# A recurrence step rearranged: one gate TANH, one spread, two f16 parts, and an f32 score product

## The chip, the cores and the metric

The kernel runs on one core of a Trainium2 chip. The metric is the device time of one launch in microseconds (us); lower is better. The kernel before took 1523.16 us, the median of three runs (1520.36 to 1537.06).

## The reference, cut to what matters

The reference is two layers over x of shape (4, 256, 512): attention over a context of 64 positions, a feed-forward with int4 weights, then a recurrent attention decoder, then a mixture of 16 experts. The decoder is a scan over the 256 positions, and each step needs the state of the one before:

```
f = conv1d(alpha, conv_w)                       # alpha: last step's attention over 64 positions
e = va . tanh(enc_proj + s @ Wa_s.T + f @ Wa_f.T + ba);  masked
alpha_new = softmax(e);   g = alpha_new @ hbatch
rec = tgt @ L_ys.T + s @ L_ss.T + g @ L_gs_w.T + L_gs_b
ig, fg, cg, og = split(rec, 4)
c_next = sig(fg) * c + sig(ig) * tanh(cg);  s_next = sig(og) * tanh(c_next)
```

Here sig(z) = 0.5 tanh(z/2) + 0.5, the batch is 4 and s, c have 64 elements each. The output y of the step is computed later from the kept histories of s and alpha.

## The kernel before, in words

Attention and the first part of the feed-forward run ahead of the recurrence. After about 302 us the 256 steps begin. The rest of the feed-forward, the inputs of the gates, the outputs and most of the experts are cut into small pieces, and `fill(...)` puts such pieces between the parts of a step on each engine. Every engine has its own instruction stream, written out by hand, in order; semaphores join them.

On TensorE a step is: the state's share of the tanh argument (L1864, high part `sh`, then low part `sl`), the state's share of the gates (L1870: five small products for each of two gate halves, over three bf16 parts of L_ss), a fill, the score maxima `eb` (L1878: eight 32-column products of `th_hi`), the exact scores `et` (L1884 twice, a fill, then L1887, three 8-column products with `th_hi` and `th_lo` as weights), a fill, the gates and sums from the exponentials (L1896, L1901, L1905, L1912, L1913), the context for the next step (L1618, three bf16 parts), the masks (L1612, L1613), a fill, the f32 convolution product (L1921, two products that each show as two instructions) and a last fill.

ScalarE makes two TANH of the 128x128 argument (L1425 to f16, L1426 to f32), two EXP (L1430, L1431), two TANH of the gates on 64 partitions each (L1439, L1440) and one of the cell (L1442). VectorE makes the state sum `rs`, `th_lo` (L1095), the maximum (L1098), `el` (L1103), the reciprocal (L1106), two normalisations, the gate sum (L1117), the spread in two halves (L1121, each with a semaphore), `ab` (L1130), the cell (L1132), `sh`, `s2` and `sl` (L1135, L1136, L1138). GpSimd copies the state (L689), does a piece of fill after `th_lo_ready`, and writes the attention history after the reciprocal.

A fill is counted in half units: a product of 256 columns is 1, one of 512 columns is 2. A credit is carried from fill to fill, so a 512-column product may overdraw it by 1 and the next fill pays. In a step the fills before `eb`, between L1884 and L1887, before L1896, before L1921 and at the end have 2, 2, 4, 4 and 3 half units. Where no work is due, `keep_busy` (L1842) issues one product of as many columns, with 384 instead of 512 for 2 half units in the first fill.

Of the kernel before, what the change touches and what calls it, by code (L numbers as in the profile page):

```python
# [17 lines left out]
P = 128  # L18
# [13 lines left out]
J = 64  # L32
# [8 lines left out]
def shape_constants():  # L41
# [6 lines left out]
    for m in range(NF // 2 + 1):  # L48
# [28 lines left out]
        "c_gatescale": np.stack([np.where(np.arange(P) < J, 1.0, 2.0), np.ones(P)], 1).astype(f32),  # L77
# [5 lines left out]
def build(nc, a, out):  # L83
    with ExitStack() as ctx:
# [31 lines left out]
        identb = sb("identb", [P, P], BF16)  # L116
# [5 lines left out]
        lss3 = sb("lss3", [J, 3, 256], BF16)  # L122
# [8 lines left out]
        vae2 = sb("vae2", [P, 2, 2 * B], F16)  # L131
# [6 lines left out]
        enc3 = sb("enc3", [P, 3, P], BF16)  # L138
# [28 lines left out]
        tfi = sb("tfi", [J, 8])  # L167
        xs = sb("xs", [J, 2, 12])
        ab = sb("ab", [J, 8])
        tc_sb = sb("tc_sb", [J, B])  # L170
# [13 lines left out]
        th_hi = ker_mem[:, 256:320].bitcast(F16)  # L184
        th_lo = ker_mem[:, 320:384].bitcast(F16)
# [69 lines left out]
        def w1_piece(q):  # L255
# [17 lines left out]
            pre_done th_s th_full th_lo_ready eb_done et_done mx_ready eh_ready ex_ready el_ready sum_done ah_done hg_done rinv_ready ahn_ready  # L273
            prod_ready g_ready q0_ready q1_ready kept tg_ready ab_ready c_ready tc_ready s_ready sh_ready sl_ready sp_done
            identb_ready hist_done part_ready
# [244 lines left out]
        def _(pool):  # L520
# [82 lines left out]
            nc.gpsimd.memset(xs[:], 0.0)  # L603
# [14 lines left out]
            nc.gpsimd.tensor_copy(identb[:], ident[:]).then_inc(s["identb_ready"], 1)  # L618
# [66 lines left out]
            for l in range(S):  # L685
# [4 lines left out]
                pool.wait_ge(s["th_lo_ready"], l + 1)  # L690
# [15 lines left out]
        def _(dve):  # L706
# [157 lines left out]
            in_parts(lss3[:], lssT[:])  # L864
# [4 lines left out]
            in_halves(vae2[:], vae[:].rearrange("p h b -> p (h b)"))  # L869
# [4 lines left out]
            in_parts(enc3[:], enc[:])  # L874
# [211 lines left out]
            for l in range(S):  # L1086
# [42 lines left out]
                dve.wait_ge(s["tg_ready"], l + 1)  # L1129
                nc.vector.scalar_tensor_tensor(ab[:], tfi[:], 1.0, xs[:, par, 0:8], ALU.add, ALU.mult).then_inc(s["ab_ready"], 1)  # L1130
# [338 lines left out]
        def _(pe):  # L1469
# [542 lines left out]
```

## Time and profile before

| | |
|---|---|
| runs (us) | 1520.36, 1523.16, 1537.06 |
| the profiled execution's own time | 1518.94 us |
| its span | 1516.8 us |
| busy share PE, PEld, DVE, ACT, POOL | 92%, 61%, 62%, 36%, 18% |
| mean granted TensorE clock | 0.93 |

PE is TensorE's matmuls, PEld its weight loads, DVE is VectorE, ACT is ScalarE, POOL is GpSimd. Matmuls are pipelined and their ends are modelled, so that a PE that shows as busy may still be waiting for its next weight load; where that happens it is seen as idle time of PEld.

### The profile page before, as it was taken

The page shows a single profiled execution, that of the slowest core. Times are in us where ns is not written, and L with a number is a line of the kernel's source. Part 1 is how long each engine was busy: PE and PEld are TensorE (multiplying, and loading weights), DVE is VectorE, ACT ScalarE, POOL GpSimd, SP SyncE. Part 2 cuts the span into 40 slices and gives each one's busy share as a digit, 9 for nine tenths or more (in the row PEclk, how much of TensorE's full clock was granted, in tenths as well). Part 3 has the DMA queues.
Part 4 walks back from the last instruction along what each step waited for, and adds up shares of the span by engine and source line. Part 5 has one row for each costly group of instructions (what it writes and reads, how often), then busy time and mean ns, then how long its engine had stood idle before and what let it go on. Part 6 is the DMA issues. An engine that isn't in the chain of part 4 may idle for free.

```text
span 1516.8 us, 43579 instructions
## 1 busy us (share of the span) xinstructions
PE 1395.5 (92%) x17408; PEld 919.4 (61%) x17408; DVE 943.9 (62%) x4478; ACT 544.3 (36%) x2143; POOL 275.1 (18%) x743
## 2 busy tenths in 40 slices
PE   4743887899999999999999999999999999999988
PEld 2533666466665676666666765556666666666546
DVE  4898455366665666675666657766655566566643
ACT  1343132134333344333334434443433333333321
POOL 3334222211111111111011111231110011111111
PEclk8565797999999999999999999999998999999989
DMA  8623000000000000000000001210000000000000
GB/s 278 240 90 90 0 1 4 1 2 2 3 2 2 2 2 2 3 2 2 2 2 2 2 19 45 58 37 2 2 16 2 2 2 9 9 2 3 9 9 14
DMA packets 19551, 37.06 MB, mean 24 GB/s; under 512 B 8436, under 2 KB 11683, under 8 KB 19348
## 3 DMA queue, kind: packets, MB, share of 16 engines
q1 hardware_dynamic: 19348, 34.28, 6.9%
q8 instruction: 136, 2.23, 0.6%
q14 instruction: 67, 0.55, 0.1%
HBM read 32.18 MB, written 2.10 MB: 23 GB/s over the span
## 4 chain that ended last, share of the span: by engine, by line
PE 83%; DVE 9%; issue 3%; ACT 2%; SPq 1%; POOL 1%; DMA 0%; DVEq 0%; ACTq 0%; POOLq 0%
PE bank L1921 9%; PE bank L1842 9%; PE bank L1635 9%; PE bank L1864 8%; PE bank L1652 6%; PE bank L1896 6%; PE bank L1673 4%; PE bank L1870 4%; PE bank L1618 3%; PE bank L1878 3%; PE bank L1905 3%; PE bank L1884 2%; PE bank L1612 2%; PE bank L1566 2%; PE bank L1518 2%
## 5 line engine op out<-in xcount | busy, mean ns | idle before, releaser
L1842 PE MATMUL bank<-ctx_lgs,identb 128*128 128x512 f16 (+2 forms) x685 | 190.9, 356 | 0.0
L1921 PE MATMUL bank<-ker_mem,uh 128*128 128x128 f32 x1020 | 184.3, 304 | 0.7 <-DVE ker_mem L1121 0.4
L1921 PEld LDWEIGHTS bank<-ker_mem,uh 128*128 128x128 f32 x1020 | 137.0, 194 | 66.1 <-DVE ker_mem L1121 48.9
L1635 PE MATMUL bank<-xT,wbig 128*128 128x256 f16 x1008 | 162.9, 275 | 0.0
L693 POOL TENSOR_TENSOR sscale<-ex,rinv 128x8 f32<-128x8 f32 x256 | 51.0, 199 | 506.8 <-DVE rinv L1106 506.8
L1439 ACT ACTIVATE xs<-gat 64x8 f32<-64x8 f32 x255 | 52.9, 207 | 244.2 <-DVE gat L1117 244.2
L1425 ACT ACTIVATE ker_mem<-bank 128x128 f16<-128x128 f32 x256 | 71.0, 278 | 184.8 <-PE bank L1864 184.8
L1430 ACT ACTIVATE eh<-bank,nmx 128x8 f16<-128x8 f32 x256 | 68.5, 268 | 172.4 <-PE bank L1887 172.4
L689 POOL COPY sscale<-s 64x4 f32<-64x4 f32 x256 | 59.0, 230 | 388.6 <-DVE s L1136 388.6
L1652 PE MATMUL bank<-wbig,interT 128*128 128x512 f16 x378 | 125.6, 399 | 0.0
L1121 DVE TENSOR_TENSOR ker_mem<-inv,ahn 128x128 f32<-128x128 f32 x510 | 124.0, 285 | 0.1
L1896 PEld LDWEIGHTS bank<-eh,ctx_lgs 128*128 128x128 f16 x2048 | 69.3, 96 | 69.9 <-ACT eh L1430 69.3
L1103 DVE TENSOR_TENSOR el<-ex,eh 128x8 f16<-128x8 f32 x256 | 42.9, 168 | 103.9 <-ACT ex L1431 103.7
L1092 DVE TENSOR_TENSOR rs<-bank,rin 128x8 f32<-128x8 f32 x256 | 42.6, 166 | 95.6 <-PE bank L1870 95.3
L1518 PE MATMUL bank<-vbd,interT 128*128 128x34 f32 x256 | 51.0, 361 | 49.2 <-ACT interT L1203 49.2
L1106 DVE RECIPROCAL rinv<-bank 128x4 f32<-128x4 f32 x256 | 46.6, 182 | 78.2 <-PE bank L1905 78.2
L1896 PE MATMUL bank<-eh,ctx_lgs 128*128 128x4 f16 x2048 | 90.3, 166 | 2.0
L1864 PEld LDWEIGHTS bank<-sh,was 64*128 64x128 f16 x512 | 28.4, 94 | 102.8 <-DVE sh L1135 98.8
L1442 ACT ACTIVATE tc_sb<-xs 64x4 f32<-64x4 f32 x255 | 52.4, 205 | 105.5 <-DVE xs L1132 105.5
L1095 DVE TENSOR_TENSOR ker_mem<-enc,ker_mem 128x128 f16<-128x128 f32 x256 | 74.8, 292 | 21.0
L1870 PE MATMUL bank<-sh,lss 64*128 64x4 f16 x1536 | 87.4, 162 | 0.0
L573 POOL TENSOR_TENSOR interT<-work,interT 128x256 f16<-128x256 f32 x84 | 56.2, 670 | 164.5 <-ACT interT L1214 93.3
(238 smaller groups left out, 3290.9 us busy)
## 6 DMA issues: line engine op xcount, KB each, us to landing
wbig<-d_gate_qT SPq DMA_DIRECT2D x4, 896.0 KB, 9.9
wbig<-d_up_qT SPq DMA_DIRECT2D x4, 896.0 KB, 20.7
wbig<-d_down_qT SPq DMA_DIRECT2D x1, 3584.0 KB, 31.5
x_sb<-d_x SPq DMA_DIRECT2D x16, 128.0 KB, 6.0
d_out<-x_sb SPq DMA_DIRECT2D x16, 128.0 KB, 2.3
sscale<-d_gate_sT SPq DMA_DIRECT2D x2, 896.0 KB, 8.3
sscale<-d_up_sT SPq DMA_DIRECT2D x2, 896.0 KB, 4.3
work<-d_g1T SPq DMA_DIRECT2D x8, 224.0 KB, 2.5
```

What stands on the lines that cost most here:

```text
L1095: nc.vector.tensor_tensor(th_lo, th, th_hi, ALU.subtract).then_inc(s["th_lo_ready"], 1)
L1121: return nc.vector.tensor_tensor(qv[:, h, :, :], inv[:].unsqueeze(1).broadcast_to([P, B, TH]), ahn[:, 4 * h:4 * h + 4].unsqueeze(2).broadc ...
L1425: nc.scalar.activation(th_hi, bank[0][:, 0:P], ACT.Tanh).then_inc(s["th_s"], 1)
L1430: nc.scalar.activation(eh[:], bank[0][:, P:P + 8], ACT.Exp, bias=nmx[:, 0:1]).then_inc(s["eh_ready"], 1)
L1518: last = mm(bank[6 + pair // 8][:, (pair % 8) * 34:(pair % 8) * 34 + 34], pT[:, n % 2, j * P:(j + 1) * P], vbd[:, b, pair // 2, :], start= ...
L1635: last = mm(tile_bank(n)[:, lo:lo + QC], w[wi][:, kt, it * P:(it + 1) * P], x_part[q % 2][xi][:, kt, :], start=(kt == 0 and wi + xi == 0), ...
L1652: last = mm(bk[:], i_part[ii][:, it, p * P:(p + 1) * P], w[wi][:, it, :], start=(it == 0 and ii + wi == 0), stop=(it == tiles - 1 and ii = ...
L1842: mm(bank[7][:, 0:n], identb[:], hg2[:, 0].rearrange("p h g -> p (h g)")[:, 0:n], start=True, stop=True)
L1864: last = mm(bank[0][:, 0:P], was2[:, j, :], st[:].unsqueeze(2).broadcast_to([J, B, TH]), start=False, stop=(st is sl), skip_group_check=True)
L1870: last = mm(bank[2][:, 4 * gp:4 * gp + 4], lss3[:, j, gp * P:(gp + 1) * P], st[:], start=(gp == 0 and j == 0 and st is sh), stop=(j == 1 a ...
L1896: mm(bank[2][:, 8 + 4 * gp:12 + 4 * gp], hg2[:, j, h, gp * P:(gp + 1) * P], e[:, 4 * h:4 * h + 4], start=False, stop=final, skip_group_che ...
L1921: mm(bank[0][:, 0:P], uh[:, h, :], qv[:, h, :, :], start=False, stop=False, skip_group_check=True)
```

## The change

The order of the gates is now i, f, c, o, as in the reference, so that one TANH over 128 partitions (into `tg`) gives all four; `ab` is made by two instructions, one on each half of the partitions. The spread is one VectorE instruction of 256 columns with one semaphore. L_ss and the context are held in two f16 parts instead of three bf16 parts. There is one TANH of the argument, in f32 (`th`); its upper two bytes, read as bf16 with a step of two, feed the maxima, and `th` itself is the weights of a single f32 score product, ahead of the fill. The fills of a TensorE step are 3, 5, 4 and 3 half units. The wait on `kept` moves from the second spread to `s2`; GpSimd's fill waits for `mx_ready`.

```diff
-            def in_parts(dst, src):
-
-                for j in range(2):
-                    link(nc.vector.tensor_copy(dst[:, j], src))
-                    link(nc.vector.tensor_tensor(src, src, dst[:, j], ALU.subtract))
-                nc.vector.tensor_copy(dst[:, 2], src).then_inc(s["part_ready"], 1)
...
-            in_parts(lss3[:], lssT[:])
+            in_halves(lss2[:], lssT[:])
...
-            in_halves(vae2[:], vae[:].rearrange("p h b -> p (h b)"))
...
-            in_parts(enc3[:], enc[:])
+            in_halves(enc2[:], enc[:])
...
+        th_top = th.bitcast(BF16).rearrange("p (n two) -> p two n", two=2)[:, 1, :]
...
-                pool.wait_ge(s["th_lo_ready"], l + 1)
+                pool.wait_ge(s["mx_ready"], l + 1)
...
-                dve.wait_ge(s["th_full"], l + 1)
-                nc.vector.tensor_tensor(th_lo, th, th_hi, ALU.subtract).then_inc(s["th_lo_ready"], 1)
-
...
-                spread(0).then_inc(s["q0_ready"], 1)
+                nc.vector.tensor_tensor(qv.rearrange("p i b t -> p (i b) t"), inv[:].unsqueeze(1).broadcast_to([P, 2 * B, TH]),
+                                        ahn[:].unsqueeze(2).broadcast_to([P, 2 * B, TH]), ALU.mult).then_inc(s["q_ready"], 1)
+
+                dve.wait_ge(s["tg_ready"], l + 1)
+                nc.vector.scalar_tensor_tensor(ab[J:P, 0:4], tg[0:J, par, 0:4], 1.0, tg[0:J, par, 4:8], ALU.add, ALU.mult)
+                nc.vector.scalar_tensor_tensor(ab[J:P, 4:8], tg[J:P, par, 0:4], 1.0, cell[J:P, par, :], ALU.add, ALU.mult).then_inc(s["ab_ready"], 1)
+                dve.wait_ge(s["ab_ready"], l + 1)
+                nc.vector.scalar_tensor_tensor(cell[J:P, 1 - par, :], ab[J:P, 4:8], 0.5, ab[J:P, 0:4], ALU.mult, ALU.add).then_inc(s["c_ready"], 1)
...
                 dve.wait_ge(s["kept"], l + 1)
-                spread(1).then_inc(s["q1_ready"], 1)
...
-                nc.scalar.activation(th_hi, bank[0][:, 0:P], ACT.Tanh).then_inc(s["th_s"], 1)
                 nc.scalar.activation(th, bank[0][:, 0:P], ACT.Tanh).then_inc(s["th_full"], 1)
...
-                nc.scalar.activation(xs[:, par, 4:12], gat[J:P, :], ACT.Tanh, scale=0.5)
-                nc.scalar.activation(tfi[:], gat[0:J, :], ACT.Tanh, scale=0.5).then_inc(s["tg_ready"], 1)
+                nc.scalar.activation(tg[:, par, :], gat[:], ACT.Tanh, scale=0.5).then_inc(s["tg_ready"], 1)
...
-                for j in range(3):
-                    mm(bank[0][:, 0:P], identb[:], enc3[:, j, :], start=(j == 0), stop=False, skip_group_check=True)
+                for j in range(2):
+                    mm(bank[0][:, 0:P], identh[:], enc2[:, j, :], start=(j == 0), stop=False, skip_group_check=True)
...
-                    for j, st in ((0, sh), (1, sh), (2, sh), (0, sl), (1, sl)):
+                    for j, st in ((0, sh), (1, sh), (0, sl)):
...
-                fill(UNIT, main_first, 384)
-                pe.wait_ge(s["th_s"], l + 1)
+                fill(UNIT + HALF_UNIT, main_first, 384)
+                pe.wait_ge(s["th_full"], l + 1)
...
-                        last = mm(bank[1][b * TH:(b + 1) * TH, h * TH:(h + 1) * TH], vah[:, h, :], th_hi[:, b * TH:(b + 1) * TH],
+                        last = mm(bank[1][b * TH:(b + 1) * TH, h * TH:(h + 1) * TH], vah[:, h, :], th_top[:, b * TH:(b + 1) * TH],
...
-                pe.wait_ge(s["th_full"], l + 1)
-                for j in range(2):
-                    mm(bank[0][:, P:P + 8], th_hi, vae2[:, j, :], start=False, stop=False, skip_group_check=True)
-                fill(UNIT, main_first)
-                pe.wait_ge(s["th_lo_ready"], l + 1)
-                mm(bank[0][:, P:P + 8], th_lo, vae2[:, 0, :], start=False, stop=True, skip_group_check=True).then_inc(s["et_done"], 1)
-
-                fill(2 * UNIT, side_first)
+                mm(bank[0][:, P:P + 8], th, vae[:].rearrange("p h b -> p (h b)"), start=False, stop=True, skip_group_check=True).then_inc(s["et_done"], 1)
+
+                fill(2 * UNIT + HALF_UNIT, side_first)
...
+                pe.wait_ge(s["q_ready"], l + 1)
                 for h in range(2):
-                    pe.wait_ge(s[f"q{h}_ready"], l + 1)
                     mm(bank[0][:, 0:P], uh[:, h, :], qv[:, h, :, :], start=False, stop=False, skip_group_check=True)
                 fill(UNIT + HALF_UNIT, side_first)
```

## Rows read from the trace of the kernel before

**Rows 1.** Page: granted clock, group of L1121 (busy us, mean ns); then the reciprocal's line.

```profile
PEclk8565797999999999999999999999998999999989
...
L1121 DVE TENSOR_TENSOR ker_mem<-inv,ahn 128x128 f32<-128x128 f32 x510 | 124.0, 285 | 0.1
...
L1106 DVE RECIPROCAL rinv<-bank x256: 181/182/184, 304.4 to 1466.1; 128x4 f32<-128x4 f32 x128
```

**Rows 2.** Timeline (start us, us, engine line op [idle before]): spread, gates, state.

```profile
800.60 0.49 DVE L1121 TENSOR_TENSOR ker_mem<-inv,ahn 128x128 f32<-128x128 f32 x2
800.71 0.21 ACT L1439 ACTIVATE xs<-gat 64x8 f32<-64x8 f32 x1 [0.87 <-DVE gat L1117]
...
800.93 0.52 PEld L1921 LDWEIGHTS bank<-ker_mem,uh 128*128 128x128 f32 x4
...
801.17 0.16 DVE L1130 SCALAR_TENSOR_TENSOR ab<-tfi,xs 64x8 f32<-64x8 f32 x1
801.37 0.15 DVE L1132 SCALAR_TENSOR_TENSOR xs<-ab 64x4 f32<-64x4 f32 x1
...
801.49 0.49 PE L1635 MATMUL bank<-xT,wbig 128*128 128x256 f16 x3
...
801.79 0.15 DVE L1135 SCALAR_TENSOR_TENSOR sh<-xs,tc_sb 64x4 f16<-64x4 f32 x1 [0.27 <-ACT tc_sb L1442]
...
802.00 0.11 PEld L1864 LDWEIGHTS bank<-sh,was 64*128 64x128 f16 x2 [0.31 <-DVE sh L1135]
...
802.13 0.42 DVE L897 SCALAR_TENSOR_TENSOR work<-work,bank 128x256 f32<-128x256 f32 x1
802.26 0.09 PEld L1864 LDWEIGHTS bank<-sl,was 64*128 64x128 f16 x1
```

**Rows 3.** Timeline of the same step: argument, maxima, scores, exponentials; the next spread.

```profile
802.53 0.28 ACT L1425 ACTIVATE ker_mem<-bank 128x128 f16<-128x128 f32 x1 [0.77 <-PE bank L1864]
...
802.65 0.39 PE L1635 MATMUL bank<-xT,wbig 128*128 128x256 f16 x2
...
802.98 0.13 PEld L1878 LDWEIGHTS bank<-ker_mem,vah 128*32 128x32 bf16 x8 [0.21 <-ACT ker_mem L1425]
...
803.14 0.11 PEld L1884 LDWEIGHTS bank<-vae,ker_mem 128*128 128x128 f16 x2
...
803.28 0.23 DVE L1098 TENSOR_REDUCE nmx<-bank 128x1 f32<-128x64 f32 x1
...
803.43 0.17 PE L1887 MATMUL bank<-vae,ker_mem 128*128 128x8 f16 x1
...
803.63 0.27 ACT L1430 ACTIVATE eh<-bank,nmx 128x8 f16<-128x8 f32 x1 [0.66 <-PE bank L1887]
...
803.95 0.27 PEld L1896 LDWEIGHTS bank<-eh,ctx_lgs 128*128 128x128 f16 x8 [0.18 <-ACT eh L1430]
...
804.31 0.11 PEld L1905 LDWEIGHTS bank<-el,onesb 128*128 128x128 bf16 x2
...
805.09 0.49 DVE L1121 TENSOR_TENSOR ker_mem<-inv,ahn 128x128 f32<-128x128 f32 x2
```

**Rows 4.** Timeline of the first step, whose first fill is one product of 384 columns.

```profile
302.44 0.28 ACT L1425 ACTIVATE ker_mem<-bank 128x128 f16<-128x128 f32 x1 [1.14 <-PE bank L1864]
...
302.56 0.34 PE L1842 MATMUL bank<-ctx_lgs,identb 128*128 128x384 f16 x1
...
302.83 0.13 PEld L1878 LDWEIGHTS bank<-ker_mem,vah 128*32 128x32 bf16 x8 [0.17 <-ACT ker_mem L1425]
```

**Rows 5.** Timeline: four f32 products of 16 columns in the router, eight weight loads.

```profile
710.27 0.97 PEld L1757 LDWEIGHTS bank<-gwT,kbd 128*128 128x128 f32 x8
```

**Rows 6.** Timeline of VectorE: reciprocals, six microseconds apart.

```profile
716.43 0.18 DVE L1106 RECIPROCAL rinv<-bank 128x4 f32<-128x4 f32 x1 [0.56 <-PE bank L1905]
...
722.39 0.18 DVE L1106 RECIPROCAL rinv<-bank 128x4 f32<-128x4 f32 x1 [0.55 <-PE bank L1905]
```

**Rows 7.** Timeline ahead of the recurrence: the down projection on TensorE.

```profile
284.83 8.74 PE L1581 MATMUL bank<-wbig,interT 128*128 128x512 f16 x38
```

More of the change, by code:

```diff
@@ L76, in shape_constants @@
         "c_time2": np.stack([np.tile(np.arange(TH), B), np.tile(np.arange(TH, T), B)]).astype(f32),
-        "c_gatescale": np.stack([np.where(np.arange(P) < J, 1.0, 2.0), np.ones(P)], 1).astype(f32),
+        "c_gatescale": np.stack([np.ones(P), np.where(np.arange(P) < J, 2.0, 1.0)], 1).astype(f32),
         "c_batchsel": (bm[None] == four).astype(f32),
@@ L166, in build @@
         sl = sb("sl", [J, B], F16)
[L167 to L170, printed above, removed]
+        tg = sb("tg", [P, 2, 8])
+        cell = sb("cell", [P, 2, B])
+        ab = sb("ab", [P, 8])
+        tc_sb = sb("tc_sb", [P, B])
         s2 = sb("s2", [J, 2, B])
@@ L272, in build @@
             vbd_zero wsel_zero setup_v setup_mm setup_cp mask_ready scale_ready
-            pre_done th_s th_full th_lo_ready eb_done et_done mx_ready eh_ready ex_ready el_ready sum_done ah_done hg_done rinv_ready ahn_ready
-            prod_ready g_ready q0_ready q1_ready kept tg_ready ab_ready c_ready tc_ready s_ready sh_ready sl_ready sp_done
-            identb_ready hist_done part_ready
+            pre_done th_full eb_done et_done mx_ready eh_ready ex_ready el_ready sum_done ah_done hg_done rinv_ready ahn_ready
+            prod_ready g_ready q_ready kept tg_ready ab_ready c_ready tc_ready s_ready sh_ready sl_ready sp_done
+            identh_ready hist_done part_ready
             split_high split_done gated upped stat_ready top_ready y_done u_ready yy_done lg_done lgx_ready pe_exp wsel_ready wt_done wT_ready wT_low_ready expert_ready""".split()
@@ L593, in _ @@
             pool.wait_ge(s["setup_in"], 16 * SETUP)
-            nc.gpsimd.tensor_scalar(lssT[:, 0:J], lssT[:, 0:J], 0.5, None, ALU.mult)
-            nc.gpsimd.tensor_scalar(lssT[:, 2 * J:4 * J], lssT[:, 2 * J:4 * J], 0.5, None, ALU.mult)
+            nc.gpsimd.tensor_scalar(lssT[:, 0:2 * J], lssT[:, 0:2 * J], 0.5, None, ALU.mult)
+            nc.gpsimd.tensor_scalar(lssT[:, 3 * J:4 * J], lssT[:, 3 * J:4 * J], 0.5, None, ALU.mult)
             nc.gpsimd.tensor_scalar(lsyT[:], lsyT[:], 0.5, None, ALU.mult)
             nc.gpsimd.tensor_scalar(wasT[:], wasT[:], 0.5, None, ALU.mult)
-            nc.gpsimd.tensor_scalar(lgsT[:, J:2 * J], lgsT[:, J:2 * J], 2.0, None, ALU.mult).then_inc(s["scale_ready"], 1)
+            nc.gpsimd.tensor_scalar(lgsT[:, 2 * J:3 * J], lgsT[:, 2 * J:3 * J], 2.0, None, ALU.mult).then_inc(s["scale_ready"], 1)
             rstd_of(10)
             rstd_of(11)
-            nc.gpsimd.memset(xs[:], 0.0)
+            nc.gpsimd.memset(cell[:], 0.0)
             nc.gpsimd.memset(s2[:], 0.0).then_inc(s["s_ready"], 1)
@@ L1606, in _ @@
             pe.wait_ge(s["rin_ready"], 2)
-            pe.wait_ge(s["part_ready"], 5)
-            pe.wait_ge(s["identb_ready"], 1)
+            pe.wait_ge(s["part_ready"], 4)
+            pe.wait_ge(s["identh_ready"], 1)
             def masks():
@@ L1840, in keep_busy @@
             def keep_busy(n):
-                mm(bank[7][:, 0:n], identb[:], hg2[:, 0].rearrange("p h g -> p (h g)")[:, 0:n], start=True, stop=True)
+                mm(bank[7][:, 0:n], identh[:], hg2[:, 0].rearrange("p h g -> p (h g)")[:, 0:n], start=True, stop=True)
             credit = [0]
@@ L1984 @@
     ctx = i["ctx_1024"]
-    perm = np.concatenate([np.arange(q * J, (q + 1) * J) for q in (1, 2, 0, 3)])
     kT = ctx.reshape(B, T, 8, HD).transpose(2, 3, 0, 1)
```

34 lines of the change are left out of this document (12 added, 22 removed).

## The prediction

> **What bounds the kernel now.** I read the page's row of granted clocks and the reciprocal's line first [rows 1]: one reciprocal a step, 256 from 304.4 to 1466.1 us, so 1161.7 us in 255 steps, 4.556 us each. The recurrence is 77% of the span, and what is saved in a step is multiplied by 255. The second view is the timeline of one step, between two spreads: 805.09 - 800.60 = 4.49 us [rows 2, 3]. The page says that PE is 92% busy, but much of that is fill, and the weight loads tell another story: L1864 sat idle 0.31 us until VectorE's `sh`, L1878 0.21 us until the TANH, L1896 0.18 us until the EXP [rows 2, 3]. So a step is a loop through four engines, in which TensorE's fills are nearly as long as the waits that they stand in. A shorter link helps only until the fill beside it is the longer one, and I price both at each place.
>
> **Gates.** Before, the first TANH starts at 800.71, the second after it, and `ab` starts at 801.17 [rows 2]. Now one TANH ends at 800.71 + 0.21 = 800.92 (8 columns on twice the partitions; bounds 0.20 and L1425's 0.28 for 128 columns), `tg` is there at 800.95. VectorE must also be done with the spread. Two halves of 0.285 took 0.49 us together [rows 1, 2], so neighbours on VectorE overlap by 0.08. A 128x256 f32 instruction takes 0.42 (L897) [rows 2]: the spread ends at 801.02, the first `ab` starts at 800.95, the second 0.08 later (upper bound: a whole 0.16). `c` starts 0.04 after the second has ended: 800.95 + 0.08 + 0.16 + 0.04 = 801.23, against 801.37. All behind it, TANH of the cell, `sh`, `s2`, `sl`, moves with it: **0.14 us**. The wait on `kept` ahead of `s2` costs nothing: the copy that it waits for was started when the last state was written, nearly a step ago.
>
> What TensorE does beside it: L1921 started at 800.93, 0.05 after the first half spread; it now waits for the whole, 801.02 + 0.05 = 801.07, **0.14 us later**. Its four instructions and the way into the fill took 801.49 - 800.93 = 0.56 us, so the last fill starts at 801.63. A 256-column product takes 0.11 us (0.49 for three, 0.39 for two [rows 2, 3]), three take 0.32: streamed out at 801.95. The new `sh` is on TensorE at 801.86, so L1864's first products start 0.09 late; but `sl`, whose load was at 802.26 and is possible now at 802.12, comes after two 128-column products, at 801.95 + 0.11 = 802.06. So the low part still sets the end, and the 0.14 stays whole, with 0.06 us to spare. With two 512-column products in the last fill (every other step of a 512-column stretch) the end is 0.11 later and 0.05 of the 0.14 is lost.
>
> If the spread takes as long as the halves did one after the other without overlap (2 x 0.285 = 0.57, upper bound [rows 1]), everything behind it moves 0.15 more, the margin is gone and the gain is 0.05; if it took 0.35 it would still be 0.14, for then the TANH sets it.
>
> **Argument and maxima.** L1870 goes from ten small products to six. They ran between L1864's low part and the fill, at about 0.035 us each: the fill starts 0.14 earlier. It is 3 half units instead of 2, +0.11: it ends 0.03 earlier. That matters: the first maxima start 0.17 us after the TANH's end behind two 256-column products (802.98 - 802.81 [rows 3]), but 0.11 behind one of 384 columns (302.83 - 302.72 [rows 4]). So **0.03 us** gained, 0.01 in steps of dummy fill; in 512-column stretches, where the first fill is now one or two products in turn, +0.07 and -0.07. The f32 TANH alone takes what the f16 one did. Reading `th` with a step of two costs the moving side between nothing and a doubling of eight times 32 columns, 0.11 us; I take nothing.
>
> **Scores.** Before, EXP starts 0.65 us after the maxima's first load, on L1887's end, 803.60; the maximum itself was done at 803.51 [rows 3]. `th_lo`'s wait and the fill in between made L1887 the last. Now the f32 product's loads start where L1884's did, 0.16 behind the maxima's. No row shows it; four f32 products of 16 columns take eight loads in 0.97 us [rows 5], 0.11 a load after a first of 0.19. Two loads are 0.30, and the second product's way out adds 0.10: done at 0.16 + 0.40 = 0.56, EXP at 0.60. Bounds: one f16 product's load and way out, 0.27, where the maximum would set EXP at 0.58; and twice the loads, 0.62, EXP at 0.82. At 0.60, **0.05 us** are gained. On TensorE the f32 product lets the fill of 5 half units start at 0.16 + 0.26 = 0.42 and end at 0.95; L1896 would be ready at 0.60 + 0.32 = 0.92 against 0.97 before. So some 0.03 to 0.05 arrive; I count 0.04. Three 512-column products there end at 1.06 and take back the 0.07 won before the maxima.
>
> The Trainium skill, page FP8 and Floating Point Precision, TensorE Precision Notes, gives a true FP32 product four passes through the array. By that rule, if each pass had its own load, the product would end 0.22 us later and the sum below would be near nothing; rows 5 show two loads a product, and the rival "dear product" carries the difference.
>
> **Costed at nothing.** The third context product is 0.05 us of TensorE between L1913 and the masks, which wait for the reciprocal anyway. `th_lo` leaves VectorE before the maximum, which waited for L1878. GpSimd's fill starts 0.2 us later, when the maximum is done; its next instruction needs the reciprocal, more than 1 us later. Nobody waits in the step for either. The eight VectorE instructions gone from the set-up, none of more columns than L897's, ran beside or ahead of the down projection, 8.74 us of unbroken TensorE [rows 7].
>
> **The sum.** Fill of 256 columns or dummy: 0.14 + 0.03 + 0.04 = 0.21. Fill of 512 columns: 0.14 and 0.09 in turn, 0.11. Of the 15 x 255 = 3825 half units, the two down projections in the loop are 378 products of 512, 756 half units, 20%. Mean 0.8 x 0.21 + 0.2 x 0.11 = 0.19; x 255 = 48 us. The mean step is 4.556 and the plain one 4.49, 17 us in all, mostly in a few steps that TensorE or a long fill sets; a tenth off for those: **44 us**. The profiled execution's own time 1518.94 becomes 1475. The median of the runs shown is 4.2 above it and the lowest 1.4; I put the median at **1477**.
>
> **Rivals.** (a) *TensorE takes it back*: one spread makes the convolution product late and the fills stay at 15 half units in a shorter step. For it: only 0.06 us of margin at `sl`, 0.03 at L1896. Against it: both margins are positive at the measured 0.42. With the upper spread 0.05 + 0.03 + 0.02 = 0.10 a step are left, 25 us: about 1494. (b) *Dear product*: the f32 loads double, EXP goes to 0.82 instead of 0.65 after the maxima and the gates' 0.14 is eaten: 1517, no change. Rows 5 speak against it. (c) *Slower, by the clock*: a step with the granted clock at half takes 722.39 - 716.43 = 5.96 us [rows 6], 1.5 more than a plain one. That stretch came after a step whose fill was the narrow f32 products of rows 5, where TensorE did less. The change takes ten small products and one of 128 columns out and puts weight loads of f32 in. If more steps fall to 1.2 GHz, 30 of them cost the whole gain and 42 make it 1% slower, about 1538. Against it: the same fill stands in a step 4% shorter, so per microsecond TensorE does no less than before, and most slices show nine tenths or more [rows 1]. (d) *It doesn't bite*: if `sl` or EXP hung on something else I have not seen, 1519.
>
> **Chances.** Forecast 0.68 (1463 to 1488), (a) 0.18, (b) 0.05, (c) 0.05, (d) 0.04. Within 1% of before, 1508 to 1538, is what a measurement can't tell from no change. Faster by over 1%: 0.68 + 0.18 less a little = 0.85; same: 0.10; slower 0.05. The range takes in (a): 1461 to 1502.
>
> **What would show it.** In the changed trace: plain steps of 4.28 us; `c` 0.63 after the spread's start against 0.77; spread 0.42; L1921's first load 0.47 after the spread's start; idle before L1864 nearly gone; EXP 0.60 after the maxima's first load; f32 score product two loads; as few slices below full clock as before. A spread near 0.57, a product of four loads, or L1896 later than 0.97 after the maxima would prove me wrong, in that order of likelihood.

## The result: slower by 1.3%, not faster by 3%

| | before | after |
|---|---|---|
| median of the runs (4 each) | 1528.12 us | 1546.95 us (1542.30 to 1551.83) |
| ratio, with its 95% interval | | 1.0128 (1.0079 to 1.0178) |
| profiled execution's own time | 1518.94 us | 1542.94 us |
| its span | 1516.8 us | 1541.2 us |
| mean granted clock | 0.93 | 0.93 |

I predicted 1477 us, a range of 1461 to 1502, and 5% for slower.

The profile after loses next to nothing outside the recurrence: first reciprocal at 304.63 us (304.4 before), last at 1490.16 (1466.1 before, [rows 1]), so 23.9 of the 24.4 us of span are in the 255 steps. I call a step under 4.8 us plain. Paired step by step, the 220 steps that are plain in both traces lose 15.8 us together, and the other 35 lose 8.1 us.

Where the plain steps lose is seen when each is cut at four points. Counted from one `sh` to the next (219 plain pairs, 15.5 us), the maxima's start costs 8.7 us, the way from there to EXP gives 8.7 back, the way from EXP to the spread costs 5.3, and the way from the spread to the cell costs 9.6. So there are three losses: the gates, the first fill, and one between EXP and spread. All three are taken in turn below, and the long steps with the experiments.

A table of medians over the plain steps, sorted by what the first fill is, shows the first two. Offsets are from the start of `sh`, in us:

| first fill, kernel | maxima's first load | EXP | spread | cell | step |
|---|---|---|---|---|---|
| 256-column products, before | 1.18 | 1.84 | 3.29 | 4.06 | 4.49 |
| same, after | 1.20 | 1.83 | 3.29 | 4.10 | 4.53 |
| 512-column products, before | 1.19 | 1.85 | 3.30 | 4.08 | 4.50 |
| same, after | 1.32 | 1.95 | 3.40 | 4.22 | 4.65 |
| dummy products, before | 1.12 | 1.78 | 3.24 | 4.00 | 4.43 |
| same, after | 1.12 | 1.74 | 3.20 | 4.01 | 4.44 |

The page after, first the clock row and the groups of the parts that I had priced. A group line gives the count, then the busy us in all and the mean ns of one, then the idle time ahead of them:

```profile
PEclk8565797999999999998999999999998999999998
...
L1421 ACT ACTIVATE tg<-gat 128x8 f32<-128x8 f32 x255 | 53.2, 209 | 252.0 <-DVE gat L1104 252.0
...
L1107 DVE TENSOR_TENSOR ker_mem<-inv,ahn 128x256 f32<-128x256 f32 x255 | 106.8, 419 | 0.2
...
L1863 PE MATMUL bank<-vae,enc 128*128 128x8 f32 x512 | 100.1, 268 | 0.0
```

All three prices were right: the TANH over 128 partitions 0.21, the spread 0.42, the f32 product two instructions. Now the timeline of one step after, with a fill of 256-column products (start us, us, engine, line, operation):

```profile
801.52 0.42 DVE L1107 TENSOR_TENSOR ker_mem<-inv,ahn 128x256 f32<-128x256 f32 x1
801.64 0.21 ACT L1421 ACTIVATE tg<-gat 128x8 f32<-128x8 f32 x1 [0.88 <-DVE gat L1104]
801.97 0.16 DVE L1111 SCALAR_TENSOR_TENSOR ab<-tg 64x4 f32<-64x4 f32 x1
801.99 0.52 PEld L1897 LDWEIGHTS bank<-ker_mem,uh 128*128 128x128 f32 x4 [0.30 <-DVE ker_mem L1107]
...
802.14 0.16 DVE L1112 SCALAR_TENSOR_TENSOR ab<-tg,cell 64x4 f32<-64x4 f32 x1
802.33 0.16 DVE L1114 SCALAR_TENSOR_TENSOR cell<-ab 64x4 f32<-64x4 f32 x1
...
802.76 0.16 DVE L1117 SCALAR_TENSOR_TENSOR sh<-tg,tc_sb 64x4 f16<-64x4 f32 x1 [0.27 <-ACT tc_sb L1423]
802.84 0.15 DVE L1119 SCALAR_TENSOR_TENSOR s<-tg,tc_sb 64x4 f32<-64x4 f32 x1
...
803.24 0.09 PEld L1845 LDWEIGHTS bank<-sl,was 64*128 64x128 f16 x1 [0.16 <-DVE sl L1121]
...
803.51 0.28 ACT L1408 ACTIVATE enc<-bank 128x128 f32<-128x128 f32 x1 [0.78 <-PE bank L1845]
...
803.53 0.50 PE L1616 MATMUL bank<-xT,wbig 128*128 128x256 f16 x3
...
803.96 0.13 PEld L1859 LDWEIGHTS bank<-enc,vah 128*32 128x32 bf16 x8 [0.21 <-ACT enc L1408]
...
804.13 0.30 PEld L1863 LDWEIGHTS bank<-vae,enc 128*128 128x128 f32 x2
804.13 0.39 PE L1863 MATMUL bank<-vae,enc 128*128 128x8 f32 x2
...
804.27 0.23 DVE L1085 TENSOR_REDUCE nmx<-bank 128x1 f32<-128x64 f32 x1 [0.46 <-PE bank L1859]
...
804.59 0.27 ACT L1412 ACTIVATE eh<-bank,nmx 128x8 f16<-128x8 f32 x1 [0.80 <-PE bank L1863]
```

Read it against rows 2. The TANH is done at 801.85, but the first `ab` starts at 801.97: not before the spread's end (801.94), though L1117 and L1121 of before had overlapped with their forerunners. The second `ab` starts 0.17 later, when the first is over; `sh` and `s2` (L1119, shown as `s`) are 0.08 apart in the same trace. So the cell comes 0.81 us after the spread's start, against 0.77 in [rows 2]; I had written 0.63. TensorE is where I said: L1897's first load 0.47 behind the spread's start.

The second loss is at the first fill, and largest in the stretches of 512-column fill:

```profile
1447.27 0.28 ACT L1408 ACTIVATE enc<-bank 128x128 f32<-128x128 f32 x1 [0.78 <-PE bank L1845]
...
1447.30 0.63 PE L1633 MATMUL bank<-wbig,interT 128*128 128x512 f16 x2
...
1447.85 0.13 PEld L1859 LDWEIGHTS bank<-enc,vah 128*32 128x32 bf16 x8 [0.45 <-ACT enc L1408]
```

The TANH is done at 1447.55; two products of 512 columns stand in front of the maxima, which start 0.30 behind it (0.17 in [rows 3]).

The third loss comes from GpSimd's fill, which now waits for the maximum (`mx_ready`) and no longer for `th_lo`. The groups of `el` on the two pages, before and after:

```profile
L1103 DVE TENSOR_TENSOR el<-ex,eh 128x8 f16<-128x8 f32 x256 | 42.9, 168 | 103.9 <-ACT ex L1431 103.7
```

```profile
L1090 DVE TENSOR_TENSOR el<-ex,eh 128x8 f16<-128x8 f32 x256 | 47.9, 187 | 95.4 <-ACT ex L1413 95.4
```

One step of each with such a piece of fill on GpSimd, before and after:

```profile
606.66 0.67 POOL L573 TENSOR_TENSOR interT<-work,interT 128x256 f16<-128x256 f32 x1 [1.12 <-DVE ker_mem L1095]
...
607.37 0.17 DVE L1103 TENSOR_TENSOR el<-ex,eh 128x8 f16<-128x8 f32 x1 [0.26 <-ACT ex L1431]
```

```profile
611.74 0.67 POOL L571 TENSOR_TENSOR interT<-work,interT 128x256 f16<-128x256 f32 x1 [1.33 <-DVE nmx L1085]
...
612.21 0.22 DVE L1090 TENSOR_TENSOR el<-ex,eh 128x8 f16<-128x8 f32 x1 [0.22 <-ACT ex L1413]
```

Before, GpSimd's instruction is over (607.33) when `el` starts. After, it ends at 612.41, and `el` ends 0.02 behind it and takes 0.22 us instead of 0.17. In the changed kernel's trace `el` takes over 0.20 us in 74 of 256 steps and ends 0.02 to 0.03 behind GpSimd in each of them; before, in 1. The spread starts 1.51 us after EXP where `el` overlaps GpSimd's fill, and 1.46 elsewhere. Of the sixteen traces, the twelve with the new wait have 71 to 76 such steps each, and the four with the old one (before, gates_only, parts_only, parts_22453) have 1 each. No run moves this wait alone.

### The profile page after: what moved, and what is told of

The parts are those of the page before. It is cut to its first block, busy times and chain, and to the rows that moved or that the text cites. A ratio compares the mean times of both kernels' runs of the same rounds, so it can differ in the third digit from the quotient of the medians.

```text
span 1541.2 us, 39817 instructions
## 1 busy us (share of the span) xinstructions
PE 1418.7 (92%) x15914; PEld 914.2 (59%) x15914; DVE 901.2 (58%) x4214; ACT 452.7 (29%) x1632; POOL 276.1 (18%) x743
## 4 chain that ended last, share of the span: by engine, by line
PE 83%; DVE 10%; issue 3%; ACT 1%; SPq 1%; POOL 1%; DMA 1%; DVEq 0%; ACTq 0%; POOLq 0%
PE bank L1897 12%; PE bank L1823 9%; PE bank L1616 8%; PE bank L1845 7%; PE bank L1633 6%; PE bank L1872 5%; PE bank L1863 5%; PE bank L1654 4%; PE bank L1859 3%; PE bank L1593 3%; PE bank L1881 3%; PE bank L1851 2%; PE bank L1599 2%; PE bank L1499 2%; PE bank L1547 2%
## 5 line engine op out<-in xcount | busy, mean ns | idle before, releaser
L1897 PEld LDWEIGHTS bank<-ker_mem,uh 128*128 128x128 f32 x1020 | 137.6, 195 | 105.4 <-DVE ker_mem L1107 105.2
L1897 PE MATMUL bank<-ker_mem,uh 128*128 128x128 f32 x1020 | 185.6, 306 | 6.4 <-DVE ker_mem L1107 2.8
L1823 PE MATMUL bank<-ctx_lgs,identh 128*128 128x512 f16 (+3 forms) x727 | 190.1, 346 | 0.0
L1085 DVE TENSOR_REDUCE nmx<-bank 128x1 f32<-128x64 f32 x256 | 57.5, 225 | 126.5 <-PE bank L1859 126.5
L1421 ACT ACTIVATE tg<-gat 128x8 f32<-128x8 f32 x255 | 53.2, 209 | 252.0 <-DVE gat L1104 252.0
L1408 ACT ACTIVATE enc<-bank 128x128 f32<-128x128 f32 x256 | 71.0, 277 | 181.9 <-PE bank L1845 181.9
L1107 DVE TENSOR_TENSOR ker_mem<-inv,ahn 128x256 f32<-128x256 f32 x255 | 106.8, 419 | 0.2
L1090 DVE TENSOR_TENSOR el<-ex,eh 128x8 f16<-128x8 f32 x256 | 47.9, 187 | 95.4 <-ACT ex L1413 95.4
L1423 ACT ACTIVATE tc_sb<-cell 64x4 f32<-64x4 f32 x255 | 51.6, 202 | 174.2 <-DVE cell L1114 174.2
L1863 PE MATMUL bank<-vae,enc 128*128 128x8 f32 x512 | 100.1, 268 | 0.0
L1616 PEld LDWEIGHTS bank<-xT,wbig 128*128 128x128 f16 x1008 | 85.8, 102 | 11.1 <-issue 1.2
## 6 DMA issues: line engine op xcount, KB each, us to landing
wbig<-d_gate_qT SPq DMA_DIRECT2D x4, 896.0 KB, 10.1
```

Source lines behind the costliest of these rows:

```text
L1107: nc.vector.tensor_tensor(qv.rearrange("p i b t -> p (i b) t"), inv[:].unsqueeze(1).broadcast_to([P, 2 * B, TH]), ahn[:].unsqueeze(2).broa ...
L1408: nc.scalar.activation(th, bank[0][:, 0:P], ACT.Tanh).then_inc(s["th_full"], 1)
L1616: last = mm(tile_bank(n)[:, lo:lo + QC], w[wi][:, kt, it * P:(it + 1) * P], x_part[q % 2][xi][:, kt, :], start=(kt == 0 and wi + xi == 0), ...
L1823: mm(bank[7][:, 0:n], identh[:], hg2[:, 0].rearrange("p h g -> p (h g)")[:, 0:n], start=True, stop=True)
L1863: mm(bank[0][:, P:P + 8], th, vae[:].rearrange("p h b -> p (h b)"), start=False, stop=True, skip_group_check=True).then_inc(s["et_done"], 1)
L1897: mm(bank[0][:, 0:P], uh[:, h, :], qv[:, h, :, :], start=False, stop=False, skip_group_check=True)
```

## The experiments

### The gates alone

```diff
 before, plus:
-                nc.scalar.activation(xs[:, par, 4:12], gat[J:P, :], ACT.Tanh, scale=0.5)
-                nc.scalar.activation(tfi[:], gat[0:J, :], ACT.Tanh, scale=0.5).then_inc(s["tg_ready"], 1)
+                nc.scalar.activation(tg[:, par, :], gat[:], ACT.Tanh, scale=0.5).then_inc(s["tg_ready"], 1)
-                nc.vector.scalar_tensor_tensor(ab[:], tfi[:], 1.0, xs[:, par, 0:8], ALU.add, ALU.mult)...
+                nc.vector.scalar_tensor_tensor(ab[J:P, 0:4], tg[0:J, par, 0:4], 1.0, tg[0:J, par, 4:8], ALU.add, ALU.mult)
+                nc.vector.scalar_tensor_tensor(ab[J:P, 4:8], tg[J:P, par, 0:4], 1.0, cell[J:P, par, :], ALU.add, ALU.mult)...
```

> The kernel before with the new gates alone (one TANH over 128 partitions, two instructions for ab), the spread still in two halves. Theory H (VectorE does not overlap an instruction with its neighbour when the start partition of an operand changes, so the second ab costs a whole instruction and the first waits for the spread's end): ab starts 0.52 us after the spread, the cell 0.88 against 0.77, a plain step 4.60 instead of 4.49, the kernel about 25 us slower than before. Theory S (the gates are fine and the single spread or the f32 product is at fault): the second ab starts 0.08 after the first, plain step 4.45 to 4.50, no slower than before.

Measured: 1573.72 us median, ratio 1.0234 (1.0144 to 1.0323). Plain steps 4.61. VectorE in one step:

```profile
802.99 0.49 DVE L1121 TENSOR_TENSOR ker_mem<-inv,ahn 128x128 f32<-128x128 f32 x2
803.10 0.21 ACT L1440 ACTIVATE tg<-gat 128x8 f32<-128x8 f32 x1 [0.84 <-DVE gat L1117]
803.50 0.15 DVE L1130 SCALAR_TENSOR_TENSOR ab<-tg 64x4 f32<-64x4 f32 x1
803.67 0.16 DVE L1131 SCALAR_TENSOR_TENSOR ab<-tg,cell 64x4 f32<-64x4 f32 x1
803.87 0.16 DVE L1133 SCALAR_TENSOR_TENSOR cell<-ab 64x4 f32<-64x4 f32 x1
```

0.51, 0.68 and 0.88 behind the spread, as theory H had it. With the spread in halves the new gates are dearer still. The plain steps lose what H said, 24.6 us in 205 of them. The other 50 lose 30.0 us more, which no theory had: the mean granted clock is below 0.9 in 29 steps, before in 9.

### The same instructions, reading from the same partition

```diff
 after, plus:
-                nc.vector.scalar_tensor_tensor(ab[J:P, 0:4], tg[0:J, par, 0:4], 1.0, tg[0:J, par, 4:8], ALU.add, ALU.mult)
+                nc.vector.scalar_tensor_tensor(ab[J:P, 0:4], tg[J:P, par, 0:4], 1.0, tg[J:P, par, 4:8], ALU.add, ALU.mult)
```

> The changed kernel, but the first ab instruction reads the upper 64 partitions like the second one (the input and cell gates are left out of the computation, the instructions are as many and as large). Theory H (a VectorE instruction whose operand starts at another partition than its neighbour's waits for that neighbour's end): the first ab still starts 0.45 us after the spread, the second 0.08 after the first instead of 0.17, the cell 0.09 earlier, a plain step 4.44 instead of 4.53, about 20 us faster than the changed kernel. Rival (two small instructions into one tile never overlap, or the step hangs elsewhere): second ab still 0.17 after the first.

Measured: 1525.91 us median, ratio to before 0.998 (0.9942 to 1.0017), 21 us under the changed kernel. Plain steps 4.48 (256), 4.55 (512) and 4.35 (dummy). One step:

```profile
805.11 0.42 DVE L1107 TENSOR_TENSOR ker_mem<-inv,ahn 128x256 f32<-128x256 f32 x1
...
805.56 0.16 DVE L1111 SCALAR_TENSOR_TENSOR ab<-tg 64x4 f32<-64x4 f32 x1
805.64 0.15 DVE L1112 SCALAR_TENSOR_TENSOR ab<-tg,cell 64x4 f32<-64x4 f32 x1
805.83 0.16 DVE L1114 SCALAR_TENSOR_TENSOR cell<-ab 64x4 f32<-64x4 f32 x1
```

The second `ab` starts 0.08 behind the first, and 223 plain steps are 20.5 us shorter together, 0.09 each, from a change of nothing but the partitions that one small instruction reads. That settles H against "two small instructions never overlap".

### The order of the two turned round

```diff
 after, plus:
-                nc.vector.scalar_tensor_tensor(ab[J:P, 0:4], tg[0:J, ...
                 nc.vector.scalar_tensor_tensor(ab[J:P, 4:8], tg[J:P, ...
+                nc.vector.scalar_tensor_tensor(ab[J:P, 0:4], tg[0:J, ...
```

> The changed kernel with the two ab instructions in the other order. Theory H: the first now reads from partition 64 where the spread read from 0, and the second goes back to 0, so both still wait: 0.45 and 0.17 as before, plain step 4.53, time unchanged. Rival theory M (only a shift between the partitions read and written breaks the overlap): the unshifted instruction now starts 0.34 to 0.37 after the spread, plain step about 4.45.

Measured: one run, 1550.42 us; plain steps 4.53 and 4.65, as in the changed kernel. The spread started at 804.41:

```profile
804.86 0.16 DVE L1111 SCALAR_TENSOR_TENSOR ab<-tg,cell 64x4 f32<-64x4 f32 x1
805.03 0.16 DVE L1112 SCALAR_TENSOR_TENSOR ab<-tg 64x4 f32<-64x4 f32 x1
```

0.45 and 0.17 again, so it is not the shift from read to written partitions that counts (theory M) but that the start changes from one instruction to the next.

The Trainium skill, page VectorE: DVE Perf Modes, section Two Vector instructions with no wait between them, states this rule: an instruction is held until all earlier ones have finished when its input or its output starts in another 32-partition quadrant than the one last read from or written to in that memory. The traces of these three kernels agree with it (0.17 from start to start where held, 0.08 where not). It spoke against the change, and I had not weighed it.

### The old gates in the changed kernel, twice

```diff
 after, with the gates of before; old_gates:
                 nc.vector.tensor_tensor(qv..., ALU.mult).then_inc(s["q0_ready"], 1)
+                dve.wait_ge(s["kept"], l + 1)
                 dve.wait_ge(s["tg_ready"], l + 1)
 old_gates_kept: the same wait ahead of s2 instead
```

> The changed kernel with the gates of before (two TANH, one ab on 64 partitions); single spread, two f16 parts, f32 score product and fills 3, 5, 4, 3 stay. Theory H: the gate chain is 0.05 us shorter than in the changed kernel, 13 us less, about 1534; the steps with fills of 512 columns stay at 4.60. Theory S: still as slow as the changed kernel, 1547. Theory C (the clock: more steps at 1.2 GHz make the loss): the time follows the count of steps over 5 us and plain steps look like before.

Measured: 1554.90 us median, ratio 1.0189 (1.0124 to 1.0254): no better than the changed kernel, which neither H nor S had. VectorE waited idle, and yet `ab` did not start until 0.10 us after the second TANH's end, where before it took 0.03:

```profile
803.90 0.42 DVE L1107 TENSOR_TENSOR ker_mem<-inv,ahn 128x256 f32<-128x256 f32 x1
...
804.23 0.21 ACT L1421 ACTIVATE tfi<-gat 64x8 f32<-64x8 f32 x1
804.54 0.16 DVE L1112 SCALAR_TENSOR_TENSOR ab<-tfi,xs 64x8 f32<-64x8 f32 x1 [0.23 <-ACT tfi L1421]
```

I had put the wait on `kept` right ahead of the one on `tg_ready`. Hence the second version.

> As old_gates, but the wait on kept stands ahead of s2, as in the changed kernel, not ahead of ab. If that extra wait in front of ab cost the 0.06 us seen there: ab 0.58 after the spread, plain steps 4.48 with 256-column fill and 4.60 with 512, 12 us less than old_gates. If the single spread itself delays ab: still 0.64 and 4.54.

Measured: 1546.28 us median, ratio 1.0118 (1.0078 to 1.0157). Plain steps 4.48 and 4.60, `ab` 0.58 after the spread: a second wait ahead of the instruction had cost 0.07 us (the cell came 0.84 after the spread, now 0.77), although its semaphore had long been up. The plain steps are the 0.05 shorter that H says. The kernel is no faster than the changed one all the same: its profiled execution loses 5.6 us against before in 216 plain steps and 25.6 us in the other 39. Nearly all of the 25.6 us are in steps at a lower clock: the mean granted clock is below 0.9 in 26 steps (9 before), and what these take above 4.5 us each comes to 35.8 us (10.1 before).

### The first fill

```diff
 after, plus:
-                fill(UNIT + HALF_UNIT, main_first, 384)
+                fill(UNIT, main_first, 384)
 ahead of the convolution product:
-                fill(2 * UNIT, side_first)
+                fill(2 * UNIT + HALF_UNIT, side_first)
```

> The changed kernel with the fills 2, 5, 5, 3 instead of 3, 5, 4, 3 half units: one half unit moved from ahead of the maxima to ahead of the convolution product. Theory F (an odd fill of 3 rounds up to two 512-column products, which hold the maxima back in every step of such a stretch): maxima 1.12 us after sh instead of 1.32 in these steps and 1.20 in steps of 256-column fill; plain steps 0.1 shorter with 512-column fill, 0.05 to 0.08 shorter with 256; 12 to 20 us faster than the changed kernel. Rival: the maxima hang on the TANH alone, or the later fill delays the convolution product by as much: within 4 us of the changed kernel.

Measured: 1523.07 us median, ratio to before 0.9931 (0.9892 to 0.9971), 24 us under the changed kernel. Maxima 1.09 and 1.10 after `sh` (even earlier than I had put it), plain steps 4.46 (256), 4.43 (512) and 4.39 (dummy). So the half unit in front of the maxima cost 25 us in 222 plain steps, more than the 20.5 us of the second `ab`'s later start. The same half unit ahead of the convolution product cost about 1 us.

### The parts alone

```diff
 before, plus:
-                for j in range(3):
-                    mm(bank[0][:, 0:P], identb[:], enc3[:, j, :], ...
+                for j in range(2):
+                    mm(bank[0][:, 0:P], identb[:], enc2[:, j, :], ...
-                    for j, st in ((0, sh), (1, sh), (2, sh), (0, sl), (1, sl)):
+                    for j, st in ((0, sh), (1, sh), (0, sl)):
```

> The kernel before with two f16 parts instead of three bf16 parts and nothing else, fills 2, 2, 4, 4, 3. Theory F (in steps with real work the maxima wait for the first fill, which starts as soon as the small products of L_ss are done): fill starts 0.14 earlier, maxima 1.10 to 1.12 after sh instead of 1.18, plain step 4.43, dummy steps 4.41 to 4.43 as before, 10 to 15 us faster than before. Rival: TensorE's small products were hidden, no change.

Measured: 1512.57 us median, ratio 0.9907 (0.9875 to 0.9938). Plain steps 4.43 with every kind of fill. One step:

```profile
800.27 0.28 ACT L1418 ACTIVATE ker_mem<-bank 128x128 f16<-128x128 f32 x1 [0.77 <-PE bank L1857]
...
800.62 0.13 PEld L1871 LDWEIGHTS bank<-ker_mem,vah 128*32 128x32 bf16 x8 [0.21 <-ACT ker_mem L1418]
...
800.96 0.22 DVE L1091 TENSOR_REDUCE nmx<-bank 128x1 f32<-128x64 f32 x1
```

The maxima now start 0.07 after the TANH, 1.08 after `sh`, but EXP stays at 1.78: it waits for the second TANH, `th_lo` and L1880, which is L1887 of before. So 0.06 of the 0.10 arrive in steps of 256-column fill, and nothing in steps of dummy fill.

### The f32 product alone, and both together

```diff
 score_2544: before, plus the one f32 TANH, th_top and
+                mm(bank[0][:, P:P + 8], th, vae[:].rearrange("p h b -> p (h b)"), ...).then_inc(s["et_done"], 1)
 with the fills 2, 5, 4, 4
 combined_2544: the same, plus the two f16 parts of parts_only
```

> The kernel before with the one f32 TANH and the f32 score product, three bf16 parts, old gates and spread in two halves, fills 2, 5, 4, 4. The f32 product makes EXP start 0.62 to 0.63 us after the maxima's first load instead of 0.66, and nothing else moves: maxima at 1.18 after sh, plain steps 4.46 against 4.49 (256-column fill), 5 to 9 us faster than before. Rival (the f32 product is a burden): plain steps of 4.49 or more, not faster.

Measured: 1538.80 us median, ratio 1.0047 (1.0006 to 1.0089), slower. The medians did as expected (EXP 0.62 after the maxima, plain steps 4.46; 4.49 with 512-column fill), but the plain steps together gain only 1.6 us in 217: what EXP gains (8.3 us) is mostly lost again between EXP and spread (5.9 us), where `el` is long in 74 steps as in the changed kernel. The other 38 steps lose 16.6 us; the mean granted clock is below 0.9 in 20 steps (9 before), and the granted clock of the stretch from 300 to 1450 us is 0.97 instead of 0.99. The first of these rows is before, the second score_2544 (after the stretch and its length: busy us of PE, PEld, DVE, ACT and POOL, then the granted clock, the DMA share and GB/s):

```profile
300.00:1450.00 1150.00, 1135.21 (x15960) 738.15 (x15959) 728.73 (x4111) 447.14 (x1963) 171.94 (x611) 0.99 0.03 8
```

```profile
300.00:1450.00 1150.00, 1141.78 (x15522) 775.14 (x15522) 658.62 (x3821) 399.58 (x1692) 171.91 (x606) 0.97 0.03 8
```

> The kernel before with only the two f16 parts and the f32 score product with one TANH, old gates and the spread in two halves, fills 2, 5, 4, 4. Theories H and F together: maxima 1.12 after sh (1.18 before), EXP 0.62 after the maxima's load (0.66), gates as before, plain steps 4.40 to 4.42 against 4.49, about 18 us faster than before. If the loss came from the f32 product or from the TANH's f32 output read with a step of two: slower than before by 5 us or more.

Measured: 1509.78 us median, ratio 0.9839 (0.9781 to 0.9896). Maxima 1.09, EXP 1.71 after `sh`, plain steps 4.40, 4.39 and 4.34. With 256-column fill the two alone shorten a step by 0.06 and 0.03 and together by 0.09, their sum. With dummy fill it is 0.00 and 0.03 alone and 0.09 together, more than the sum: the parts let the maxima start early, and the f32 product takes away the `th_lo` chain on which EXP then hung. It was run again beside others:

> combined_2544 once more beside the others on one chip: ratio to before 0.984, between 0.978 and 0.990; plain steps 4.40 with 256-column fill and 4.39 with 512.

Measured: 1514.13 us median, ratio 0.9884 (0.9813 to 0.9955), the expected ratio within its interval; plain steps 4.40, 4.39, 4.34. Against before, 222 plain steps gain 19.0 us and the other 33 give 13.5 back.

### Half of the spread on GpSimd

```diff
 combined_2544 with the new gates, plus (GpSimd, ahead of the history):
+                    pool.wait_ge(s["ahn_ready"], l + 1)
+                    nc.gpsimd.tensor_tensor(qv[:, 1, :, :], inv[:]..., ahn[:, 4:8]..., ALU.mult).then_inc(s["q1_ready"], 1)
 and 2 half units of fill behind each convolution product
```

> As combined_2544, with the new single gate TANH, and the second half of the spread made by GpSimd instead of VectorE, the last fill split to 2 half units behind each convolution product. Then VectorE is free when the TANH ends: ab 0.35 after the spread's start, second ab 0.52, cell 0.71 against 0.77 in combined_2544, plain step 4.35 instead of 4.40, 10 us faster than combined_2544. Rival: GpSimd's half takes over 0.6 us or shares VectorE's port, the second convolution product comes late and the step is longer than 4.40.

Measured: 1523.88 us median, ratio 0.9972 (0.9936 to 1.0009), plain steps 4.41 and 4.39: no gain over combined_2544.

```profile
801.15 0.28 DVE L1112 TENSOR_TENSOR ker_mem<-inv,ahn 128x128 f32<-128x128 f32 x1
801.18 0.51 POOL L692 TENSOR_TENSOR ker_mem<-inv,ahn 128x128 f32<-128x128 f32 x1 [0.89 <-DVE ahn L1106]
...
801.51 0.20 DVE L1119 SCALAR_TENSOR_TENSOR ab<-tg 64x4 f32<-64x4 f32 x1
801.72 0.16 DVE L1120 SCALAR_TENSOR_TENSOR ab<-tg,cell 64x4 f32<-64x4 f32 x1
801.92 0.16 DVE L1122 SCALAR_TENSOR_TENSOR cell<-ab 64x4 f32<-64x4 f32 x1
```

GpSimd's half takes 0.51 us in this step, and the first `ab`, beside it, takes 0.20 instead of 0.16: it ends 0.02 behind GpSimd's half, as `el` did. With the second held behind it the cell is at 0.77 after the spread, exactly where the old gates have it.

### More fill, for the clock

All three add one half unit ahead of the convolution product, 16 a step:

```diff
 after_3553: after; combined_2554: combined_2544; parts_22453: parts_only
-                fill(2 * UNIT, side_first)
+                fill(2 * UNIT + HALF_UNIT, side_first)
```

> The changed kernel with one half unit more of fill ahead of the convolution product, where TensorE sat idle 0.3 us or more: 16 instead of 15 half units a step. Theory C (about 8 us of the changed kernel's loss lies in steps in which the granted clock is 1.2 GHz, because TensorE does less in each step): plain steps stay at 4.53 and 4.65, steps over 4.8 us cost less, mean granted clock 0.935 or more, 5 to 10 us faster than the changed kernel. Rival: the longer steps come from long fill instructions on VectorE and ScalarE and not from the clock: time and clock unchanged, or longer by up to 10 us through the later convolution product.

Measured: 1543.60 us median, ratio 1.0103 (1.0067 to 1.0139), with an interval that overlaps the changed kernel's; plain steps 4.53 and 4.65. The granted clock of the stretch rose from 0.98 to 0.99, but paired with the changed kernel the steps over 4.8 us give back only 2.4 us and the plain ones lose 1.6. Inconclusive for the changed kernel: 3 us is what I can't tell from nothing here.

> combined_2544 with 16 half units. Theory C: its plain steps were 4.40, 19 us less than before in all, but 14 to 19 us were given back in steps at the lower clock; more fill ahead of the convolution product takes half of that back: mean clock 0.93, about 1502. Against it: 5 half units there end 0.06 after the spread's first half is ready, and three 512-column products 0.17 after it, so plain steps could grow to 4.43 to 4.45 and eat it: 1510.

Measured: 1498.46 us median, ratio 0.9799 (0.9734 to 0.9863). The first row is combined_2544, the second this one:

```profile
300.00:1450.00 1150.00, 1141.94 (x14462) 752.19 (x14462) 664.73 (x3870) 404.66 (x1711) 173.59 (x613) 0.96 0.03 8
```

```profile
300.00:1450.00 1150.00, 1142.28 (x14779) 758.90 (x14780) 671.62 (x3909) 409.56 (x1735) 174.34 (x619) 0.99 0.03 8
```

Its 223 plain steps pair with those of combined_2544 to 0.5 us, and the other 32 are 22.4 us shorter (17.1 against combined_again). The mean granted clock is below 0.9 in 8 steps instead of 23 and 22. In these traces the giving back was the clock, and one half unit more of fill undoes it. The medians are 11 and 16 us apart, but the intervals of the three ratios overlap, so the size is less sure than the pairing makes it look. One reason is the part ahead of the recurrence, which is the same code in all three: its first reciprocal comes at 306.2 us here and at 298.9 and 299.1 in the other two traces. It is also the version that beats both kernels: by 2.0% the kernel before, by its ratio, and its median lies 3.1% under that of the changed kernel.

> parts_only with one half unit more ahead of the convolution product, 16 in all. Theory C: plain steps 4.43 to 4.46, mean clock 0.935 or more instead of 0.926, within 5 us of parts_only on either side; slower than it by more than 5 us would say that the fill there is already on the path.

Measured: 1507.17 us median, ratio 0.9884 (0.9811 to 0.9956); plain steps 4.43. No slower than parts_only, and no faster that its interval could show: there the clock was 0.98 without it.

## Why the prediction was wrong, by its own steps

- **Gates.** The TANH (0.21), the spread (0.42) and TensorE's start (0.47) came out as written. The step that failed is "the first `ab` starts at 800.95, the second 0.08 later": I took the overlap of two neighbours that read and write from the same partition and gave it to two that do not. The cell came 0.81 after the spread, not 0.63, and +0.04 us a step stands where I had -0.14. ab_same_start shows that alone: 0.09 a step, 20.5 us in 223 steps. My upper bound for the second `ab`, "a whole 0.16", was the true value; the first `ab` starting 0.07 before the spread's end had no such bound, and the gate term as a whole had no bound of the other sign.
- **Argument and maxima.** "The fill starts 0.14 earlier" was 0.10: it starts 803.53 - 803.24 = 0.29 after `sl`'s load, against 802.65 - 802.26 = 0.39 in [rows 2, 3]. With +0.11 for the third half unit that is +0.01 to +0.02, not -0.03. For the 512-column stretches, "the first fill is now one or two products in turn" was wrong outright: the dummy product of the last fill pays exactly the credit that is left, so that the first fill starts a step with no debt and rounds 3 up to two products each time. +0.13 instead of +0.07 and -0.07 in turn. fill_2553 takes the half unit away and has the maxima at 1.10.
- **Scores.** Expected EXP 0.60 after the maxima's load, measured 0.62 to 0.63: 0.03 of the 0.05 arrive. Rival (b), the dear product, is out: two loads, 0.30 us, 0.39 with the way out. How many passes the product makes through the array no row shows.
- **Rival (c), the clock.** It was the right sign, for part of it: 8.1 of 23.9 us are in the 35 pairs that are not plain. I had argued that a shorter step makes TensorE denser; the plain step got longer. In the changed kernel's trace the mean granted clock is below 0.9 in 11 steps, before in 9, and these take 15.3 us above 4.5 us each, before 10.1. So some 5 of the 8 us lie in steps at the lower clock, and the rest in long steps at full clock (7.2 against 4.7 us). That more fill takes such steps away is shown for the combined kernels (22.4 us), not for the changed one, where it bought at most 3 us.
- **Rival (a)**, TensorE takes it back at `sl` and L1896, never came up: `sl`'s load was still 0.47 to 0.48 behind `sh`, and the first load from `eh` (L1896) 0.32 behind EXP, in both kernels. The gates never got as fast as I had put them; in ab_same_start, with the cell at 0.72, `sl`'s load is still at 0.48.
- **Costed at nothing.** The set-up (first reciprocal 0.2 us later) and the third context product: right, nothing is seen of them. GpSimd's later fill was wrong. "Nobody waits in the step for either" looked only at who needs its result; but it now runs beside `el`, which ends with it. `el` takes 5.0 us more in all, and the plain steps lose 5.3 us between EXP and spread. The medians hide this, since it is 74 steps of 256.
- **The size of it.** For plain steps the sum was -0.21 (256-column fill) and is +0.04: 0.18 of the difference from the gates, 0.05 from the first fill, 0.01 from EXP. For 512-column fill it was -0.11 and is +0.15: 0.13 to 0.18 from the gates and 0.13 from the first fill, less 0.04 that EXP gained and that I had not counted there. The GpSimd steps come on top, as a part of all steps.

What stays open: why the granted clock falls in more steps in score_2544 (20), old_gates_kept (26) and gates_only (29) than before (9), with the same 15 half units. The f32 product can't be the whole of it, for gates_only doesn't have it. Nothing here separates the kinds of TensorE work. Untested is the best version with GpSimd's fill released early, at the TANH.

## What to carry to other kernels

In a chain of small VectorE instructions, count as overlapping only those that start reading and writing where their forerunner did; one wide instruction on the engine ahead is not worth two such small ones behind it. Where waits are filled with pieces of other work, the fill in front of the wait that sets the step must be checked in the grain of the largest piece, rounding and carried credit included. An instruction moved on GpSimd can lengthen the VectorE instruction that it now stands beside, though neither needs the other's result. And when a step gets shorter but the kernel does not, compare the granted clock first: here one half unit more of fill a step made the recurrence of the combined kernel 17 to 22 us shorter in the traces (11 to 16 us in the medians), and next to nothing for parts_only.

## What the runs showed of the hardware that was not expected

- A change of the partition at which VectorE reads costs 0.09 us between small instructions: 0.17 from start to start instead of 0.08.
- A wait that is long fulfilled, put in front of another that is not, delayed the instruction by 0.07 us (0.10 instead of 0.03 behind the releaser).
- A VectorE instruction of 128x8 beside a running GpSimd instruction of 128x256 ended 0.02 to 0.03 us behind it in every one of 74 steps, and took 0.21 us or more instead of 0.17. Beside one of 128x1 (15 steps) it took its 0.17.
- The same kernel's runs follow its mean granted clock: fill_2553 took 1507.81 us at 0.935 and 1526.52 at 0.915. Part of that lies ahead of the recurrence: the same code there takes 304.6 us in the changed kernel's trace and 312.7 us in fill_2553's, with a granted clock of 0.83 and 0.75 from 150 to 300 us.
- Taking four of ten small products of four columns away moved what stands behind them by 0.10 us. With it and one context product fewer, parts_only is 0.9% faster than before.
